# One batch's first keys and queries ahead of the last one's transposed maxima, three of four row copies on ScalarE, and layer 0's first loads on two queues

## The chip, the cores and the metric

The kernel runs on one core of one Trainium2 chip. The metric is the device time of one execution in microseconds (us), the median of several runs. Engines are named as in the profile: PE is TensorE's matmul queue, PEld its weight loads, DVE is VectorE, ACT is ScalarE, POOL is GpSimd, and SP is SyncE, which here only issues DMAs (SPq in rows).

## The reference, cut to what matters

```python
# layer 0: x (16, 256, 128), for each tile of 32 positions of every batch row
xn = layernorm(x)                       # the projections q, k, v, f, beta, gate from it
q, k, v = silu(x @ Wq), silu(x @ Wk), silu(x @ Wv)
f, gate = x @ Wf1 @ Wf2, x @ Wog1 @ Wog2
def step(S, inp):                       # 256 positions, one after the other
    bS = einsum('bhk,bhkv->bhv', b_t, S)
    S = exp(g)[..., None] * S + a_t[..., None] * bS[:, :, None, :] + k_t[..., None] * v_t[:, :, None, :]
    return S, einsum('bhk,bhkv->bhv', q_t, S)
# and 64 small experts with a group-limited router on the same normalised x
# layer 1: rotary queries and keys, 16 heads of 8, causal softmax attention per batch,
# and 16 experts with a top-3 router; out = x2 + silu(experts) * attention
```

## The kernel before

**Layer 0** works on eight tiles of 32 positions. For a tile, DVE makes a layer norm (`layer_norm`, stages 0 to 5), PE transposes it and `project` makes 648 columns of projections in 3-pass split matmuls (`split3`), units k = 0 to 5: unit 0 and 1 hold the narrow rest (136 columns) of four row blocks, unit 1 also the router's logits (12 matmuls of 64 columns), units 2 to 5 the 512 wide columns. ACT copies each unit into `zs`, SP stores it to HBM in 16 DMAs (`pass_z`) and loads it back in another layout (`zr`), ACT applies the nonlinearities (`recurrence_inputs`), DVE makes coefficients and then runs the 32 steps of the recurrence (`step`, nine DVE instructions each). Tile 0 has no earlier tile to hide its preparation behind. Ahead of it, PE transposes the factors `Wf1`, `Wog1` and multiplies them with `Wf2`, `Wog2` (semaphores `s_w1t_ps`, `s_w1t`, `s_w12_ps`), and DVE splits the projection weights `wp` and router weights `wr` in a high and a low part (`s_wp`). All loads stand on SP's queue, and PE, ACT and DVE wait for all 13 small ones (`s_small`) before anything else. DVE first widens the selectors `sel`, then splits the weights, then norms x. POOL splits the expert weights; from its fourth chunk on it waits for the prepared coefficients of tile 0 (`s_pq`), and SP's later chunk loads and the load of tile 1's x stand behind those splits in its order.

**Layer 1** first runs its experts in eight tiles. Then comes **attention**, one batch after the other, 16 in all, in a software pipeline written out by hand: the function `both(ba, bx, bo, ...)` stands on PE, ACT and DVE with the same places i = 0 to 17, and interleaves batch ba's keys, queries and row maxima (`a_unit`, the table `UNITS`), batch bx's transposed scores and exp (`scores_t`, `x_unit` at `X_AT`) and values (`values` at `V_AT`), and batch bo's output (`o_unit` at `O_TB` ... `O_END`). Each engine runs its list strictly in this order and waits on semaphores between.

- `k0`, `q0`, `k1`, `q1`: four matmuls each into banks 0 or 1; ACT copies the keys to `kr`, DVE the queries to `qr`; DVE masks keys (`masked_keys`), ACT masks queries (`masked_queries`, two ACTIVATEs at places 4, 7, 10, 13).
- `max` (12): scores in banks 2 and 3 for the row maxima, reduced by DVE.
- `v`: values' projection, from a copy of the latent (`ckv_b`) made by ACT at place 0.
- `m`: when the maxima are split (`mhl`), PE transposes them into banks 2 and 3, and four copies of 2 x 1024 elements (`max_rows`) put them into the queries' spare rows: two on ACT, then two on DVE (`s_mq`). The first `max` of the next batch and the first `scores_t` of this one wait for both.
- `scores_t` of one unit waits for the exp of the one before it (one bank pair); `values` 0 waits for the last output, `s_done`, which DVE signals at `O_END`.

Of the kernel before, what the change touches and what calls it, by code (L numbers as in the profile page):

```python
# [112 lines left out]
def layer0(nc, d, scratch, sem, area):  # L113

    z_dram, y_dram, g_dram = scratch
    with ExitStack() as ctx:
# [68 lines left out]
        s_small = sem("small_weights_loaded")  # L185
# [79 lines left out]
        SMALL = 13  # L265
# [9 lines left out]
        def _(sp):  # L275
# [37 lines left out]
            def pass_z(t, par, later):  # L313
# [21 lines left out]
            pass_z(0, 0, False)  # L335
# [178 lines left out]
        def _(act):  # L514
            act.wait_ge(s_eps, 2)

            act.wait_ge(s_small, SMALL * 16)
            act.activation(wp[:, :, ZB], wbeta[:, :], ACT.Copy).then_inc(s_w12, 1)
            act.wait_ge(s_w1t_ps, 1)
            act.activation(wf1T[:, :, :], pb[0:HD0, 0, 0:2 * P].rearrange("p (a b) -> p a b", a=2), ACT.Copy).then_inc(s_w1t, 1)  # L520
            act.wait_ge(s_w12_ps, 1)
            for a, at in ((0, ZF), (1, ZG)):
                act.activation(wp[:, :, at:at + HD0], pb[:, 2, D * a:D * (a + 1)].rearrange("p (h c) -> p h c", h=H0),
                               ACT.Copy).then_inc(s_w12, 1)

            def norm(t):

                act.wait_ge(s_xc, t + 1)
                act.activation(xn[:, :, :], xc[:, :, :], ACT.Square).then_inc(s_sq, 1)
                act.wait_ge(s_var, t + 1)  # L530
                act.activation(stat[:, 1, :], stat[:, 0, :], ACT.Sqrt, bias=eps[:, 0:1], scale=1.0 / D).then_inc(s_std, 1)

            def project(t, par, k, side):
# [10 lines left out]
                elif k == 1:  # L544
                    act.activation(zs[:, 3, WIDE:ZW], bank[:, 0:REST], ACT.Copy).then_inc(s_zc, 1)
                    act.activation(scores, bank[:, 256:512].rearrange("p (s e) -> p s e", s=NS), ACT.Sigmoid).then_inc(s_sc, 1)
# [35 lines left out]
            def tile(t, par, first, ahead):  # L582
# [3 lines left out]
                for r in range(SLOTS):  # L586
                    p, what = r // 3, r % 3
                    n = P if p < PAIRS else F0
                    if ahead and r == NORM_SLOT:
                        norm(t + 1)  # L590
# [25 lines left out]
            norm(0)  # L616
            for k in range(-1, UNITS):
                project(0, 0, k, k % 4)
# [15 lines left out]
        def _(pe):  # L634
# [15 lines left out]
            pe.wait_ge(s_wp, 4)  # L650

            def project(t, par, k, side):
# [15 lines left out]
                elif k == 1:  # L668
                    split3(bank[:, 0:REST], hi[:, sub[3]], lo[:, sub[3]], wp_hi[:, WIDE:ZW], wp_lo[:, WIDE:ZW])
                    for s in range(NS):  # L670
                        last = split3(bank[:, 256 + E0 * s:256 + E0 * (s + 1)], hi[:, sub[s]], lo[:, sub[s]], wr_hi[:, :], wr_lo[:, :], first=False)
# [1317 lines left out]
```

## Time and profile before

| | before |
|---|---|
| median of 3 runs | 2104.19 us (2104.09 to 2106.93) |
| the profiled execution: time, span | 2104.4 us, 2102.7 us |
| PE, DVE, ACT, POOL busy, share of the span | 78%, 76%, 54%, 48% |
| layer 0 up to the first recurrence step | 0 to 72.9 us |
| layer 0's tiles, layer 1's experts | to about 1178 us, to about 1721 us |
| attention, 16 batches | about 1722 us to the end |
| from one batch's transposed maxima on PE to the next one's | 22.07 us (1893.08 to 1915.15) |

A row of the timeline is: start us, duration us, engine, line, operation, out<-in, count of merged instructions, and in brackets how long the engine was idle before it and what released it. Where several instructions are merged, the duration runs to the end of the last one, so the distance to the next start is what one costs its engine. The 1.7 us between span and time lie outside of the profiled span.

### The profile page before, as it was taken

The numbers are of one execution on the slowest core, as the hardware profiler recorded it, in microseconds if no ns is written. First come the engines' busy times: TensorE is split into PE (matmuls) and PEld (weight loads), VectorE is DVE, ScalarE is ACT, GpSimd is POOL, SyncE is SP. The second block draws the span as 40 slices with busy tenths as digits, with TensorE's granted clock in tenths as the row PEclk, the third lists the DMA queues.
The fourth block names the chain that finished last, engine by engine and source line by source line (L and its number), as shares of the span: only waits on it lengthen the run. The fifth ranks groups of instructions, "written<-read, shape, count | busy, mean of one in ns | idle before, by whom it ended". The sixth has DMA issues, their size and how long they took to land. (4 is left out here: it accounts for less than half of the span.)

```text
span 2102.7 us, 32686 instructions
## 1 busy us (share of the span) xinstructions
PE 1635.4 (78%) x8418; PEld 1185.5 (56%) x8418; DVE 1603.5 (76%) x4329; ACT 1137.1 (54%) x1811; POOL 1018.5 (48%) x1108
## 2 busy tenths in 40 slices
PE   3286787886868768778787399898999997888886
PEld 2164454554545436445454298787988875555554
DVE  3499999999999999999999535444344457777774
ACT  1365464564645646546454154444555447777774
POOL 2577778686787877887887400000000002332332
PEclk9598898897978988989898599999999999999998
DMA  5420020110200202002001411001110010000000
GB/s 83 108 56 1 1 66 1 25 43 1 66 0 4 63 2 51 15 0 61 1 11 38 103 21 26 19 14 27 21 26 11 11 31 9 15 22 15 22 15 13
DMA packets 140707, 58.82 MB, mean 28 GB/s; under 512 B 94743, under 2 KB 135180, under 8 KB 140556
## 3 DMA queue, kind: packets, MB, share of 16 engines
q1 hardware_dynamic: 140556, 57.19, 12.1%
q8 instruction: 48, 0.79, 0.2%
q14 instruction: 103, 0.84, 0.1%
HBM read 36.05 MB, written 21.10 MB: 27 GB/s over the span
## 5 line engine op out<-in xcount | busy, mean ns | idle before, releaser
L612 ACT ACTIVATE shared_rings<-pb 128x512 f32<-128x512 f32 (+1 forms) x784 | 434.7, 598 | 360.6 <-PE pb L639 318.4
L688 PE MATMUL pb<-hid,shared_down 128*128 128x512 f32 x528 | 308.0, 669 | 159.7 <-POOL hid L490 157.1
L486 POOL TENSOR_TENSOR hid<-shared_rings 128x512 f32<-128x512 f32 x256 | 333.9, 1304 | 178.6 <-ACT shared_rings L612 164.2
L490 POOL TENSOR_TENSOR hid<-hid,shared_rings 128x512 f32<-128x512 f32 x256 | 329.6, 1288 | 20.6 <-POOL hid L486 1.0
L1818 DVE SCALAR_TENSOR_TENSOR l_acc<-l_pb,l_gtok,l_acc 128x128 f32<-128x128 f32 x512 | 144.3, 344 | 256.1 <-PE l_pb L1462 256.1
L637 PE MATMUL pb<-xt_hi,shared_hi 128*128 128x512 f32 (+1 forms) x264 | 192.3, 729 | 101.6 <-ACT shared_rings L612 101.6
L1373 ACT ACTIVATE l_hid<-l_pb,l_cols 128x512 f32<-128x512 f32 x256 | 169.3, 688 | 182.8 <-PE l_pb L1462 182.5
L1462 PEld LDWEIGHTS l_pb<-l_big,l_hid 128*128 128x128 f32 x2048 | 247.1, 192 | 10.6
L1462 PE MATMUL l_pb<-l_big,l_hid 128*128 128x128 f32 x2048 | 247.9, 275 | 0.0
L1287 POOL TENSOR_TENSOR l_ql<-l_rope,l_qh 128x512 f32 x8 | 10.3, 1286 | 459.4 <-ACT l_qh L1367 459.4
L688 PEld LDWEIGHTS pb<-hid,shared_down 128*128 128x128 f32 x528 | 101.1, 207 | 217.0 <-POOL hid L490 191.3
L1462 PE MATMUL l_pb<-l_xt,shared_hi 128*128 128x512 f32 x512 | 176.3, 426 | 19.7 <-DVE l_rope L1750 17.9
L950 DVE TENSOR_TENSOR products<-zr,rs 128x512 f32<-128x512 f32 x256 | 174.7, 682 | 10.2 <-issue 5.7
L953 DVE TENSOR_REDUCE rs<-products 128x32 f32<-128x512 f32 x256 | 176.0, 687 | 0.0
L951 DVE TENSOR_TENSOR products<-zr,rs 128x512 f32<-128x512 f32 x256 | 174.2, 681 | 0.0
L1861 DVE TENSOR_REDUCE l_mrow<-l_pb 128x2 f32<-128x512 f32 (+1 forms) x192 | 128.1, 687 | 58.8 <-PE l_pb L1462 58.4
L637 PEld LDWEIGHTS pb<-xt_hi,shared_hi 128*128 128x128 f32 (+1 forms) x264 | 54.4, 206 | 175.3 <-ACT shared_rings L612 88.1
L1299 POOL TENSOR_TENSOR l_turnstile<-l_turnstile 128x1 f32<-128x1 f32 x128 | 24.9, 195 | 254.3 <-ACT l_big L1421 189.6
L746 PE MATMUL pb<-cwt,sel 128*128 128x512 f32 x256 | 105.5, 412 | 19.2 <-ACT cwt L562 19.2
L638 PE MATMUL pb<-xt_lo,shared_hi 128*128 128x512 f32 (+1 forms) x264 | 112.4, 426 | 0.0
L639 PE MATMUL pb<-xt_hi,shared_lo 128*128 128x512 f32 (+1 forms) x264 | 111.8, 424 | 0.0
L637 PE MATMUL pb<-xt_hi,wu_hi 128*128 128x512 f32 (+1 forms) x264 | 111.2, 421 | 0.0
(319 smaller groups left out, 3803.7 us busy)
## 6 DMA issues: line engine op xcount, KB each, us to landing
z_scratch<-zs SPq DMA_DIRECT2D x128, 81.0 KB, 3.0
zr<-z_scratch SPq DMA_DIRECT2D x8, 1296.0 KB, 8.0
x_sb<-in_L_attn_x_dram SPq DMA_DIRECT2D x32, 64.0 KB, 2.0
shared_rings<-in_L_ffn_We_gate_dram SPq DMA_DIRECT2D x4, 512.0 KB, 5.8
shared_rings<-in_L_ffn_We_up_dram SPq DMA_DIRECT2D x4, 512.0 KB, 6.9
g_scratch<-zs SPq DMA_DIRECT2D x8, 256.0 KB, 2.8
y_scratch<-yo SPq DMA_DIRECT2D x8, 256.0 KB, 2.1
shared_down<-in_L_ffn_W_dram SPq DMA_DIRECT2D x4, 512.0 KB, 5.6
```

Source lines behind the costliest of these rows:

```text
L486: pool.tensor_tensor(hid1[:, :], g, u, ALU.mult).then_inc(s_h1, 1)
L490: pool.tensor_tensor(hid[:, (p + par) % 2, :], hid1[:, :], c, ALU.mult).then_inc(s_h, 1)
L612: act.activation(dst, pb[0:n, what, :], ACT.Silu if what == 0 else ACT.Copy).then_inc(s_ev, 1)
L637: pe.matmul(out, l_hi, r_hi, start=first, stop=False, skip_group_check=True)
L688: last = pe.matmul(pb[:, SUM, :], wd[0:n, p, :], hid[0:n, (p + par) % 2, :], start=(p == 0), stop=(p == PAIRS), skip_group_check=True)
L950: dve.tensor_tensor(products[:, 2:4], two(ZG), twice, ALU.mult).then_inc(s_st, 1)
L951: dve.tensor_tensor(products[:, 0:2], two(ZF), twice, ALU.mult).then_inc(s_st, 1)
L953: dve.tensor_reduce(rs[:, 3, 0:2], products[:, 2:4], AX.X, ALU.add).then_inc(s_st, 1)
L1373: act.activation(hid[:, r % HR, :], pb[:, 2 + r % 3, :], ACT.Relu, bias=cols[:, r:r + 1]).then_inc(s_hid, 1)
L1462: return pe.matmul(out, l, r, start=start, stop=stop, skip_group_check=True)
L1818: dve.scalar_tensor_tensor(out=acc[:, s, :], in0=pb[:, 5 + e % 2, sub], scalar=gtok[par][:, s, e:e + 1], in1=acc[:, s, :], op0=ALU.mult, o ...
L1861: dve.tensor_reduce(dst, pb[:, 2 + m % 2, :].rearrange("p (j n) -> p j n", j=heads), AX.X, ALU.max).then_inc(s_ua_dve, 1)
```

## The change

**Layer 0.** SP keeps x, the identity and the four factors (now `s_small`, five loads). ACT's queue issues the projection weights and beta (`s_heads`) and the router's constants (`s_late`), eight loads, as its first instructions. The layer norm of tile 0 goes first on DVE, then the weights' split, then `sel`. Tile 0's router matmuls come after all projections, into another bank, and ACT issues the last four of the 16 stores of `zs` itself, ahead of the router's sigmoid.

**Attention.** The unit `m` leaves the table: `max_transposed` (PE) and `max_in_queries` (ACT, DVE) now run at place 2 of the next call of `both`, behind `k0` and `q0` of the next batch. ACT copies three rows, DVE one. The latent's copy goes from place 0 to 14. The first `scores_t`/`x_unit` go from places 3 and 4 to 4 and 5 (`X_AT`), the first masked keys from 1 to 2, and the whole output unit one place on, `O_END` from 7 to 8.

```diff
-        SMALL = 13
+        SMALL, HEADS, LATE = 5, 4, 4
@@ sync: x, ident, wf1, wf2 stay; onehot, tri, bias64, gate_w, wp, wbeta go; pass_z(0, 0, False, True)
                     sp.wait_ge(s_zc, t * UNITS + (s + 3))
+                    if alone and s == NS - 1:
+                        continue
@@ scalar
+            for at, name in ((ZQ, "L0_attn_Wq"), (ZK, "L0_attn_Wk"), (ZV, "L0_attn_Wv")):
+                act.dma_start(wp[:, :, at:at + HD0], d[name].rearrange("i (h c) -> i h c", h=H0)).then_inc(s_heads, 16)
+            act.dma_start(wbeta[:, :], d["L0_attn_Wbeta"]).then_inc(s_heads, 16)
...
-            norm(0)
+            act.wait_ge(s_eps, 2)
+            norm(0, True)
+            head_weights()
             for k in range(-1, UNITS):
-                project(0, 0, k, k % 4)
+                project(0, 0, k, k % 4, True)
+            act.wait_ge(s_zc, UNITS)
+            for b in range(BS):
+                act.dma_start(z_dram[0, NS - 1, b].rearrange("h n c -> n h c"),
+                              zs[TP * b:TP * (b + 1), NS - 1, :].rearrange("p (h c) -> p h c", h=H0)).then_inc(s_zst, 16)
+            act.wait_ge(s_lg, 1)
+            router_scores(pb[:, SUM, :])
@@ vector
-            for stage in range(6):
+            for stage in range(5):
                 layer_norm(0, 0, stage)
+            head_weights()
+            layer_norm(0, 0, 5)
+            dve.wait_ge(s_late, LATE * 16)
+            dve.tensor_copy(sel[:, :, :], over(onehot[:, :], F0)).then_inc(s_sel, 1)
@@ layer 1, attention
-        UNITS = ["k0", "q0", "k1", "q1"] + ["max"] * 12 + ["v", "m"]
+        UNITS = ["k0", "q0", "k1", "q1"] + ["max"] * 12 + ["v"]
+        PLACES, MAX_AT, LATENT_AT, ROWS_BY_ACT = NU + 1, 2, 14, 3
-        QUERIES_AT, KEYS_AT = {4: (0, 0), 7: (0, 2), 10: (1, 0), 13: (1, 2)}, {1: (0, 0, 4), 5: (1, 0, 2), 7: (1, 2, 2)}
-        X_AT, V_AT = (3, 4, 6, 7, 9, 10, 12, 13), (9, 11, 14, 17)
-        RAW_AT, O_TB, O_NORM, O_OT, O_WO, O_END = 17, 1, 2, 4, 6, 7
+        QUERIES_AT, KEYS_AT = {4: (0, 0), 7: (0, 2), 10: (1, 0), 13: (1, 2)}, {2: (0, 0, 4), 5: (1, 0, 2), 7: (1, 2, 2)}
+        X_AT, V_AT = (4, 5, 6, 7, 9, 10, 12, 13), (9, 11, 14, 17)
+        RAW_AT, O_TB, O_NORM, O_OT, O_WO, O_END = 17, 2, 3, 5, 7, 8
@@ scalar
+            def max_in_queries(b, par):
+                act.wait_ge(s_mt, b + 1)
+                act.wait_ge(s_qb, (b + 1) * 4)
+                for j in range(ROWS_BY_ACT):
+                    last = act.activation(max_rows(par, j), pb[32 * j:32 * j + 2, 2:4, :].rearrange("p a (g n) -> p (a g) n", n=N), ACT.Copy)
+                last.then_inc(s_mq[0], 1)
...
-                for i in range(NU):
+                for i in range(PLACES):
                     if bo is not None:
                         o_unit(bo, i)
+                    if bx is not None and i == MAX_AT:
+                        max_in_queries(bx, px)
```

How the instructions stand shows on ACT at the turn from one batch to the next. Before, `l_pb` to `shared_hi` (line 1402) are the copies of the transposed maxima, `shared_down` to `l_big` is the latent, line 1393 copies keys 0 and keys 1, and line 1421 is the first exp:

```order
L1399 REGISTER_ALU
L1400 ISA [waits a_unit_in_psum]
L1402 ACTIVATE shared_hi<-l_pb 2x4x256 [waits a_queries_masked]
L1402 ACTIVATE shared_hi<-l_pb 2x4x256
L1389 ISA
L1389 ACTIVATE l_big<-shared_down 33x256
L1391 ISA
L1393 ACTIVATE l_wqk<-l_pb,shared_rings 128x512 [waits a_unit_in_psum]
L1391 REGISTER_ALU
L1393 ACTIVATE l_wqk<-l_pb,shared_rings 128x512 [waits a_unit_in_psum]
L1417 ISA
L1421 ACTIVATE l_big<-l_pb 128x768 [waits a_probs_used,a_scoresT_in_psum]
```

Now line 1429 is a copy of keys, line 1440 the three rows of maxima, line 1450 a masked query and line 1459 the first exp:

```order
L1427 ISA
L1429 ACTIVATE l_wqk<-l_pb,shared_rings 128x512 [waits a_unit_in_psum]
L1438 REGISTER_ALU [waits a_max_transposed]
L1440 ACTIVATE shared_hi<-l_pb 2x4x256 [waits a_queries_masked]
L1440 ACTIVATE shared_hi<-l_pb 2x4x256 x2
L1427 REGISTER_ALU
L1429 ACTIVATE l_wqk<-l_pb,shared_rings 128x512 [waits a_unit_in_psum]
L1446 ISA
L1450 ACTIVATE shared_lo<-l_xt,shared_rings 128x2x256 [waits a_unit_read_by_dve]
L1450 ACTIVATE shared_lo<-l_xt,shared_rings 128x2x256
L1455 ISA
L1459 ACTIVATE l_big<-l_pb 128x768 [waits a_probs_used,a_scoresT_in_psum]
```

Keys 0 stand ahead of the maxima and keys 1 behind them, the latent's copy is gone from here, and two masked queries now stand between keys 1 and the first exp.

On DVE the places 6 to 8 are these; lines 1861 and 1898 are the reductions of maxima, 1875 and 1920 masked keys, and the waits on `a_wo_in_psum` and after it are the output's last two operations. Before:

```order
L1848 REGISTER_ALU
L1861 TENSOR_REDUCE l_mrow<-l_pb 128x2 [waits a_unit_in_psum]
L1891 ISA [waits a_wo_in_psum]
L1892 TENSOR_TENSOR shared_rings<-l_pb,shared_rings 128x256 [waits a_gate1_loaded0]
L1895 REGISTER_ALU [waits a_x2_loaded0,a_final_chain]
L1896 TENSOR_TENSOR shared_rings<-shared_rings 128x256 [waits a_out_stored]
L1848 REGISTER_ALU
L1861 TENSOR_REDUCE l_mrow<-l_pb 128x4 [waits a_unit_in_psum]
L1875 TENSOR_SCALAR l_kb<-l_xt,shared_rings 128x2x256 [waits a_unit_read_by_act]
L1875 TENSOR_SCALAR l_kb<-l_xt,shared_rings 128x2x256
```

and now:

```order
L1885 REGISTER_ALU
L1898 TENSOR_REDUCE l_mrow<-l_pb 128x4 [waits a_unit_in_psum]
L1920 TENSOR_SCALAR l_kb<-l_xt,shared_rings 128x2x256 [waits a_unit_read_by_act]
L1920 TENSOR_SCALAR l_kb<-l_xt,shared_rings 128x2x256
L1936 ISA [waits a_wo_in_psum]
L1937 TENSOR_TENSOR shared_rings<-l_pb,shared_rings 128x256 [waits a_gate1_loaded0]
L1940 REGISTER_ALU [waits a_x2_loaded0,a_final_chain]
L1941 TENSOR_TENSOR shared_rings<-shared_rings 128x256 [waits a_out_stored]
L1885 REGISTER_ALU
L1898 TENSOR_REDUCE l_mrow<-l_pb 128x2 [waits a_unit_in_psum]
```

The output's last two operations have gone behind one more reduction and two masked keys.

On PE, behind the last values of a batch (line 1632 before, 1673 now), the transposes of the maxima are line 1588 before and 1650 now, `l_kh` to `l_ql` are keys 0 and queries 0 of the next batch. Before:

```order
L1588 MATMUL l_pb<-shared_rings,l_mhl 128x128 [waits a_max_split]
L1588 MATMUL l_pb<-shared_rings,l_mhl 128x128 x7
L1672 UNCONDITIONAL_BRANCH
L1672 ISA
L1462 ISA [waits a_unit_read_by_act]
L1462 MATMUL l_pb<-l_kh,l_rep 128x256
L1462 REGISTER_ALU
L1462 MATMUL l_pb<-l_kl,l_rep 128x256
L1462 MATMUL l_pb<-l_kh,l_rep 128x256
L1462 MATMUL l_pb<-l_kl,l_rep 128x256
L1639 REGISTER_ALU
L1643 MATMUL l_pb<-shared_rings,l_rope 128x128 [waits a_raw_out_copied]
```

and now:

```order
L1502 MATMUL l_pb<-l_kl,l_rep 128x256
L1502 MATMUL l_pb<-l_kh,l_rep 128x256
L1502 MATMUL l_pb<-l_kl,l_rep 128x256
L1625 REGISTER_ALU
L1502 REGISTER_ALU [waits a_unit_read_by_dve]
L1502 MATMUL l_pb<-l_qh,l_rep 128x256
L1502 REGISTER_ALU
L1502 MATMUL l_pb<-l_ql,l_rep 128x256
L1502 MATMUL l_pb<-l_qh,l_rep 128x256
L1502 MATMUL l_pb<-l_ql,l_rep 128x256
L1650 MATMUL l_pb<-shared_rings,l_mhl 128x128 [waits a_max_split]
L1650 MATMUL l_pb<-shared_rings,l_mhl 128x128 x7
```

Eight matmuls of the next batch now run ahead of the transposes, and keys 1 and the transposes of the raw output (`l_rope`) stand behind them.

## Rows read from the trace of the kernel before

**Rows 1.** Windows: busy time of each engine in one tile of layer 0.

```profile
211.00:349.00 138.00, 102.22 (x344) 66.15 (x344) 136.02 (x376) 76.90 (x129) 108.61 (x87) 0.87 0.11 26
```

**Rows 2.** Timeline of layer 0's start: loads, weights, layer norm, first projection.

```profile
9.15 0.66 SPq L295 DMA_DIRECT2D wbeta<-in_L_attn_Wbeta_dram  x1
...
11.44 2.29 DVE L780 CAST sel<-onehot 128x4096 fp32r<-128x4096 f32 x1 [10.21 <-DMA wbeta<-in_L_attn_Wbeta_dram]
...
15.05 0.85 DVE L783 CAST wp_hi<-products 128x648 fp32r<-128x648 f32 x1 [1.31 <-ACT products L523]
...
18.84 0.68 DVE L793 TENSOR_REDUCE rs<-x_sb 128x4 f32<-128x512 f32 x1
...
20.92 1.28 ACT L531 ACT_TABLE_LOAD   x1
...
26.20 0.45 PE L637 MATMUL pb<-wp_hi,xt_hi 128*128 128x136 f32 x1 [1.51 <-DVE xt_lo L810]
```

**Rows 3.** Timeline, the first wide projection, its stores and the load back.

```profile
31.31 0.77 PE L637 MATMUL pb<-wp_hi,xt_hi 128*128 128x512 f32 x1
...
34.03 8.36 SPq L322 DMA_DIRECT2D z_scratch<-zs  x16
...
47.95 0.56 SPq L325 DMA_DIRECT2D zr<-z_scratch  x1
...
56.12 0.65 ACT L567 ACTIVATE zr<-zr 128x512 f32<-128x512 f32 x1 [19.96 <-DMA zr<-z_scratch]
```

**Rows 4.** Timeline of DVE: the first recurrence step.

```profile
72.91 0.69 DVE L950 TENSOR_TENSOR products<-zr,rs 128x512 f32<-128x512 f32 x1
```

**Rows 5.** Timeline of ACT in one batch of attention, window from 1889 us.

```profile
1894.29 2.04 ACT L1402 ACTIVATE shared_lo<-l_pb 2x1024 fp32r<-2x1024 f32 x2 [0.39 <-PE l_pb L1588]
...
1898.32 0.69 ACT L1393 ACTIVATE l_xt<-l_pb,shared_rings 128x512 fp32r<-128x512 f32 x1 [0.83 <-PE l_pb L1462]
1898.91 0.80 ACT L1421 ACTIVATE l_big<-l_pb 128x768 f32<-128x768 f32 x1
1899.60 1.33 ACT L1412 ACTIVATE shared_hi<-l_xt,shared_rings 128x512 fp32r<-128x512 f32 x2
1900.82 0.81 ACT L1421 ACTIVATE l_big<-l_pb 128x768 f32<-128x768 f32 x1
1901.51 0.39 ACT L1432 ACTIVATE l_big<-l_pb 128x256 f32<-128x256 f32 x1
1902.33 0.81 ACT L1421 ACTIVATE l_big<-l_pb 128x768 f32<-128x768 f32 x1 [0.43 <-PE l_pb L1462]
```

**Rows 6.** Timeline of DVE in the same batch: output, reduction, masked keys.

```profile
1904.19 0.41 DVE L1892 TENSOR_TENSOR shared_rings<-l_pb,shared_rings 128x256 f32<-128x256 f32 x1
1904.74 0.42 DVE L1896 TENSOR_TENSOR shared_rings<-shared_rings 128x256 f32<-128x256 f32 x1
1905.08 0.68 DVE L1861 TENSOR_REDUCE l_mrow<-l_pb 128x4 f32<-128x512 f32 x1
1905.68 1.05 DVE L1875 TENSOR_SCALAR l_kb<-l_xt,shared_rings 128x512 fp32r<-128x512 f32 x2
```

**Rows 7.** Timeline of PE in the same batch.

```profile
1891.96 0.86 PE L1632 MATMUL l_pb<-l_front_rows,l_hid 128*32 128x256 f32 x16
1893.08 1.09 PE L1588 MATMUL l_pb<-shared_rings,l_mhl 128*128 128x128 f32 x8 [0.27 <-DVE l_mhl L1866]
...
1901.68 0.62 PE L1462 MATMUL l_pb<-shared_lo,l_wqk 128*128 128x512 f32 x2 [0.27 <-ACT l_big L1421]
1902.13 0.38 PE L1462 MATMUL l_pb<-shared_rings,l_big 128*128 128x128 f32 x2
...
1905.67 0.86 PE L1632 MATMUL l_pb<-l_big,l_hid 128*32 128x256 f32 x16
```

**Rows 8.** Attention's last stretch by windows, and PE's timeline in it.

```profile
2078.00:2084.00 6.00, 4.53 (x17) 3.53 (x18) 0.85 (x2) 2.71 (x4) 2.95 (x11) 0.54 0.00 0
...
2079.42 1.01 PE L1462 MATMUL l_pb<-shared_lo,l_wqk 128*128 128x512 f32 x2 [0.57 <-ACT l_big L1421]
```

The columns of a windows row are: the stretch, its length, then busy us and instructions of PE, PEld, DVE, ACT and POOL, the granted clock of PE, the busy share of the DMA engines and GB/s.

More of the change, by code:

```diff
@@ L514, in _ @@
         def _(act):
[L515 to L524, printed above, removed]
@@ L528, in norm, with router_scores @@
+            def norm(t, alone):
                 act.wait_ge(s_xc, t + 1)
                 act.activation(xn[:, :, :], xc[:, :, :], ACT.Square).then_inc(s_sq, 1)
+                if alone:
+                    factors()
                 act.wait_ge(s_var, t + 1)
                 act.activation(stat[:, 1, :], stat[:, 0, :], ACT.Sqrt, bias=eps[:, 0:1], scale=1.0 / D).then_inc(s_std, 1)
-            def project(t, par, k, side):
+            def router_scores(bank):
+                act.activation(scores, bank[:, 256:512].rearrange("p (s e) -> p s e", s=NS), ACT.Sigmoid).then_inc(s_sc, 1)
@@ L535, in project @@
+            def project(t, par, k, side, alone=False):
                 bank = pb[:, side, :]
@@ L545, in project @@
                     act.activation(zs[:, 3, WIDE:ZW], bank[:, 0:REST], ACT.Copy).then_inc(s_zc, 1)
-                    act.activation(scores, bank[:, 256:512].rearrange("p (s e) -> p s e", s=NS), ACT.Sigmoid).then_inc(s_sc, 1)
+                    if not alone:
+                        router_scores(bank)
                 else:
@@ L668, in project @@
                 elif k == 1:
-                    split3(bank[:, 0:REST], hi[:, sub[3]], lo[:, sub[3]], wp_hi[:, WIDE:ZW], wp_lo[:, WIDE:ZW])
-                    for s in range(NS):
-                        last = split3(bank[:, 256 + E0 * s:256 + E0 * (s + 1)], hi[:, sub[s]], lo[:, sub[s]], wr_hi[:, :], wr_lo[:, :], first=False)
+                    last = split3(bank[:, 0:REST], hi[:, sub[3]], lo[:, sub[3]], wp_hi[:, WIDE:ZW], wp_lo[:, WIDE:ZW])
+                    if not alone:
+                        last = router(par, bank, False)
                 else:
@@ L675, in project, with router @@
                 last.then_inc(s_zp, 1)
+            def router(par, bank, first):
+                for s in range(NS):
+                    sub = slice(P * s, P * (s + 1))
+                    last = split3(bank[:, 256 + E0 * s:256 + E0 * (s + 1)], xt_hi[par][:, sub], xt_lo[par][:, sub], wr_hi[:, :], wr_lo[:, :], first=first and s == 0)
+                return last
             def router_weights(t):
@@ L1658, in both @@
             def both(ba, bx, bo_, pa, px, po):
-                for i in range(NU):
+                for i in range(PLACES):
+                    if bx is not None and i == MAX_AT:
+                        max_transposed(bx)
                     if bx is not None and i in X_AT:
```

132 lines of the change are left out of this document (69 added, 63 removed).

## The prediction

> **What bounds the kernel now.** I read the stages first, by windows. In a tile of layer 0 DVE is busy 136.0 of 138 us [rows 1]: the recurrence sets that stage, so it ends as much sooner as its first step starts sooner, and nothing else there matters. Layer 1's experts are not touched. In attention no engine is full, so there the order of the instructions and their waits decide, and I followed one batch of the timeline on all three engines.
>
> The start is one serial chain. SP has issued its last small load at 9.15, and everybody waits for it: DVE's selectors start at 11.44 [rows 2]. DVE then splits the weights (15.05 to 18.8), only then norms x (from 18.84), and PE projects from 26.20 [rows 2]. The stores of the projections are issued from 34.03, the load back is issued at 47.95, when the last store has landed, and lands at 56.12, when ACT goes on after 20 us of idling [rows 3]. The first step stands at 72.91 [rows 4].
>
> A batch of attention has this chain. Values of the last batch on PE (1891.96), transposed maxima (1893.08) [rows 7], row copies on ACT (1894.29), two keys' copies, exp 0 at 1898.91, masked queries at 1899.60, exp 1 at 1900.82, the output's copy at 1901.51, exp 2 at 1902.33 [rows 5], the output's product on DVE at 1904.19 and its sum at 1904.74 [rows 6], and only after that sum the new values on PE at 1905.67 [rows 7]. Behind them in PE's order stand all remaining scores for maxima, which DVE needs to reach the next transposes. The same point comes again 22.07 us later (the table of times).
>
> **Layer 0's start.** x and the five factor loads stay ahead on SP. A small load is used 2.3 us after its issue begins (9.15 to 11.44) [rows 2]; x is issued first, before 2.7 us, so it is there at about 5.0. From 18.84 to 26.20 the norm, the transposes and their split take 7.4 [rows 2]. Put into that path are the split of the weights, 3.8 (15.05 to 18.84) less some 1.5 in which PE transposes x and ACT copies it anyway, so 2.3, and a table load of 1.3 ahead of ACT's first square (duration of the load at 20.92) [rows 2]; the selectors' 2.3 leave it. That gives 5.0 + 7.4 + 2.3 + 1.3 = 16.0 for the first projection, 10.2 sooner. ACT's queue was not used for loads before: if its eight issues cost what SP's cost, 0.7 each, they end at 6.4 and are early; if both queues shared one issuing unit, the factors would come as late as 11.4 as before, the first projection at about 19, 7.0 sooner. I take the first, since each engine's issues are instructions of its own.
>
> From 26.20 to 31.31 PE runs 24 narrow matmuls, 0.213 each [rows 2, 3]. Twelve of them, the router's, go behind the wide ones: 2.6 less before the first store, which is issued at 34.03 - 10.2 - 2.6 = 21.2. SP spends 8.36 on 16 issues, 0.52 each, and the last store lands 13.9 after the first issue [rows 3]. With four of them on ACT, SP's twelve end 2.1 sooner, so the load back is issued at 21.2 + 11.8 = 33.0. If the transfers and not the issues set the pace, this 2.1 is lost. The Trainium skill, DMA: Bandwidth & Descriptors (Issuing engines are not separate DMA queues), says just that: DMAs of all queues end on the same 16 engines and a second queue saves only the issuing time. By that rule alone the saving would be 12.8, by the row it is 14.9. I stay with 14.9. The load back takes 8.2 as before, so ACT goes on at 41.2 in place of 56.12: **14.9 us**. The router's sigmoid now comes behind ACT's four issues and the twelve matmuls, some 5 us of the 20 that ACT idled: hidden. Everything after (POOL's later splits, SP's chunk loads, tile 1's x) hangs on the coefficients of tile 0, so it moves along, and the first step is at 58.0. Bounds: 9.6 (shared issuing, 7.0 + 2.6, and nothing from the stores) and 17 (the last store lands 2 us sooner because fewer queue behind each other).
>
> **Attention.** I count from PE's values, 1891.96, as zero and move each step by pitches of the same rows. Before: transposes at 1.12, row copies 2.33, exp 0 6.95, exp 1 8.86, output copy 9.55, exp 2 10.37, product 12.23, new values 13.71.
>
> - Transposes: they waited for DVE's maxima until 1.12. Now the values (0.8 of PE) are followed by keys 0 and queries 0, eight matmuls. The nearest rows bound them by 0.4 (sixteen of the values' take 0.86) and 1.8 (two scores take 0.45, 1901.68 to 1902.13) [rows 7]; I take 1.1, between the two, as they have half the columns of a score: transposes at 1.9, so 0.8 later, row copies at 3.15.
> - Row copies on ACT: two took 2.04 [rows 5], three take 3.06 and end at 6.2. DVE's part shrinks by a row, but both counts are waited for, and ACT's is last. Before, ACT still had the latent's copy and keys 0 behind its rows, which are now elsewhere; keys 1 follow directly (pitch 0.6) and end at 6.8.
> - Exp 0 now has a masked pair of queries ahead of it, 1.22 (1899.60 to 1900.82) [rows 5]: 8.0 in place of 6.95, **1.05 later**. The three pieces nearly cancel up to there; what is left is the pair.
> - Exp 1: the next scores start 0.86 after an exp starts (1900.82 to 1901.68) and the exp 0.65 after that [rows 5, 7]. Before, this hid behind the masked pair; now it stands open: 8.0 + 1.5 = 9.5. Exp 2 the same, 11.0, 0.63 later than before.
> - The output's copy stood between exp 1 and exp 2, in ACT's idle time. At place 7 it comes behind exp 2: 11.0 + 0.69 = 11.7, **2.15 later**. Its matmuls on PE come 0.62 behind it (1901.51 to 1902.13) [rows 5, 7], at 12.3, and take 0.8.
> - DVE's product and sum, places 8 in place of 7, now wait for one more reduction and a masked pair of keys ahead of them: that reduction needs PE's matmul behind the output's, 13.1 + 0.75, then 0.6 and 1.0 [rows 6]: product at 15.45 (before 12.23), sum at 16.0, done at 16.45. The values, 13.71 before, start at 16.45, **2.75 later**. The fifth scores, just ahead of them on PE, come about 1 later, with exp 3, so they are not what is waited for.
> - Behind the values the order is as before. About 0.3 comes back, because DVE has already masked its keys when the next maxima are there. So the next batch's values come **2.45 us** later, 24.5 in place of 22.1.
>
> Fourteen calls of `both` carry all three batches: 14 x 2.45 = 34.3. In the first and the last ones the same places apply in part; I add 1.5. Attention: +36, bounds +28 and +42 by moving each of the pitches by a tenth.
>
> **Sum.** The profiled execution took 2104.4, as good as the median 2104.19. 2104.4 - 14.9 + 34.3 + 1.5 = **2125**. Its own range with the bounds above: 2104.4 - 17 + 28 to 2104.4 - 9.6 + 42, 2115 to 2137.
>
> **The rivals.**
> - *The output's delay is harmless* (other side). If the new values don't wait for the sum, because ACT or PE get there early by the moved latent copy and the earlier keys, only small changes are left in attention. For it: masked keys end about 1 us sooner, so the first maxima could start sooner. Against it: PE's list has the second scores ahead of the second maximum, and these wait for exp 0. Price: the head alone, 2089. It decides for faster as soon as a batch costs less than 1.05 more (14.9 / 14). Chance 0.17.
> - *Half of it*: a batch costs about 1.1 more, since only exp 0's delay remains: 2104.4 - 14.9 + 15.4 = 2105. Chance 0.07.
> - *PE's clock falls.* A batch would have three gaps of about 1.6 us (before the scores 0 and 1 and the values) where one was. In attention's last stretch, with such gaps, the granted clock is 0.54, mostly the lower level of 1.2 GHz, and a score pair takes 1.01 in place of 0.62 [rows 7, 8]. Each of some five rounds of scores and exp would cost 0.4 more, 2.0 a batch, 28 in all: 2153. The Trainium skill, TensorE: Matmul & The Clock Gate (Why this matters for your kernels), warns of idle gaps between bursts of matmuls, and the row agrees. Chance 0.14, and half-way cases are in the range.
> - *The start gives less*: one issuing unit for both queues, 9.6 us: 2131. Chance 0.1, inside of the main case's range.
> - The forecast, 2115 to 2137, has the remaining 0.52 and these 0.1.
>
> **How the numbers follow.** The likeliest is 2125. The range must leave out no more than 0.2: the first rival is left out, the half case and the fallen clock are taken in: 2100 to 2154. A measurement of this kernel tells about 0.2%, 4 us, from no change. Faster by more: 0.18; within: 0.05, from the half case; slower: 0.77.
>
> **What would show it.** Right: ACT's first nonlinearity on zr near 41 and the first step near 58; PE's transposed maxima 24 to 25 us apart from batch to batch; on PE the values of place 9 waiting for DVE's sum, with 1 to 2 us of idle time; ACT's output copy behind the third exp; an open gap of about 0.8 on ACT before exp 1 and exp 2. Wrong: a batch of 22 or less, values waiting for POOL or for nothing, or a load back that is issued later than 36.

## The result and the profile after

| | before | changed |
|---|---|---|
| median, 4 runs each on the same chip | 2105.56 us | 2144.03 us (2142.87 to 2147.72) |
| ratio | | 1.0186, 95% interval 1.0168 to 1.0203 |
| the profiled execution: time, span | 2104.4, 2102.7 us | 2143.75, 2141.7 us |
| first recurrence step of layer 0 | 72.91 | 61.17 |
| first transposed maxima of attention | 1736.34 | 1726.23 |
| mean distance of the 16 transposed maxima | 22.42 | 25.66 |

The kernel is 38.5 us slower; the forecast was 20.8 slower (2125 against 2104.2), with a range up to 2154. The page of the profile shows where to look. These are its busy time and its granted clock in 40 slices; the last eight slices are attention. The clock row of the kernel before stands below them.

```profile
span 2141.7 us, 32651 instructions
...
PE 1654.1 (77%) x8418; PEld 1203.1 (56%) x8418; DVE 1587.0 (74%) x4313; ACT 1152.2 (54%) x1827; POOL 1024.2 (48%) x1108
...
PEclk7697898988988889889896899999999988999997
```

```profile
PEclk9598898897978988989898599999999999999998
```

PE runs as many instructions as before (8418) and is busy longer with them (1654.1 against 1635.4 us), and the first two slices of attention have dropped to an eight. That is a hint, no more, as a nine covers everything from 0.90 up. The windows below show it plainly.

The timeline of the start, by the places of [rows 2 to 4]: layer norm on DVE, its table load on ACT, the first projection on PE, the first store on SP and the four on ACT's queue, the load back, ACT on zr, the first step.

```profile
6.11 0.69 DVE L822 TENSOR_REDUCE rs<-x_sb 128x4 f32<-128x512 f32 x1 [4.88 <-DMA x_sb<-in_L_attn_x_dram]
...
7.61 1.28 ACT L536 ACT_TABLE_LOAD   x1 [7.61 <-DVE xc L825]
...
16.67 0.45 PE L658 MATMUL pb<-wp_hi,xt_hi 128*128 128x136 f32 x1 [3.16 <-DVE xt_lo L839]
...
21.51 6.37 SPq L319 DMA_DIRECT2D z_scratch<-zs  x12
...
24.75 2.02 ACTq L636 DMA_DIRECT2D z_scratch<-zs  x4
...
36.13 0.67 SPq L322 DMA_DIRECT2D zr<-z_scratch  x1
...
44.37 0.65 ACT L580 ACTIVATE zr<-zr 128x512 f32<-128x512 f32 x1 [15.91 <-DMA zr<-z_scratch]
...
61.17 0.69 DVE L979 TENSOR_TENSOR products<-zr,rs 128x512 f32<-128x512 f32 x1
```

Up to the first store the sum is nearly as forecast (21.51 against 21.2). From there to the load back it takes 14.6 us, not the 11.8 of the forecast and not less than the 13.9 of before [rows 3]. The load back is issued at 36.13, just past the 36 that the forecast had named as a sign of being wrong. The first step is 11.7 sooner, not 14.9.

One batch of attention, by the places of [rows 5 to 7]. First ACT's timeline: row copies, keys 1, masked pair, exp 0, 1 and 2, the output's copy.

```profile
1908.15 3.07 ACT L1440 ACTIVATE shared_lo<-l_pb 2x1024 fp32r<-2x1024 f32 x3 [0.47 <-PE l_pb L1650]
1911.25 0.69 ACT L1429 ACTIVATE l_xt<-l_pb,shared_rings 128x512 fp32r<-128x512 f32 x1
1911.84 1.32 ACT L1450 ACTIVATE shared_hi<-l_xt,shared_rings 128x512 fp32r<-128x512 f32 x2
1913.06 0.80 ACT L1459 ACTIVATE l_big<-l_pb 128x768 f32<-128x768 f32 x1
1914.72 0.81 ACT L1459 ACTIVATE l_big<-l_pb 128x768 f32<-128x768 f32 x1 [0.86 <-PE l_pb L1502]
1916.63 0.81 ACT L1459 ACTIVATE l_big<-l_pb 128x768 f32<-128x768 f32 x1 [1.10 <-PE l_pb L1502]
1917.33 0.38 ACT L1470 ACTIVATE l_big<-l_pb 128x256 f32<-128x256 f32 x1
```

Then DVE's: masked keys, the output's product and its sum.

```profile
1920.16 1.13 DVE L1920 TENSOR_SCALAR l_kb<-l_xt,shared_rings 128x512 fp32r<-128x512 f32 x2
1921.21 0.41 DVE L1937 TENSOR_TENSOR shared_rings<-l_pb,shared_rings 128x256 f32<-128x256 f32 x1
1921.75 0.65 DVE L1941 TENSOR_TENSOR shared_rings<-shared_rings 128x256 f32<-128x256 f32 x1
```

And PE's: the last values of the batch before (the zero of the count), the transposed maxima, scores 0, 1, 2 and 3, the new values, and the next transposed maxima.

```profile
1905.16 0.86 PE L1673 MATMUL l_pb<-l_front_rows,l_hid 128*32 128x256 f32 x16
...
1907.00 1.03 PE L1650 MATMUL l_pb<-shared_rings,l_mhl 128*128 128x128 f32 x8
...
1911.36 0.61 PE L1502 MATMUL l_pb<-shared_lo,l_wqk 128*128 128x512 f32 x2 [1.50 <-ACT shared_lo L1440]
...
1913.91 0.77 PE L1502 MATMUL l_pb<-shared_lo,l_wqk 128*128 128x512 f32 x2 [1.48 <-ACT l_big L1459]
...
1915.58 1.01 PE L1502 MATMUL l_pb<-shared_lo,l_wqk 128*128 128x512 f32 x2
...
1917.49 0.67 PE L1502 MATMUL l_pb<-shared_lo,l_wqk 128*128 128x512 f32 x2 [0.23 <-ACT l_big L1459]
...
1922.55 0.86 PE L1673 MATMUL l_pb<-l_big,l_hid 128*32 128x256 f32 x16 [2.25 <-DVE shared_rings L1941]
...
1932.36 1.03 PE L1650 MATMUL l_pb<-shared_rings,l_mhl 128*128 128x128 f32 x8
```

The three gaps on PE are there: 1.50 and 1.48 ahead of scores 0 and 1, and one ahead of the values, which DVE's sum ends, as forecast. That third gap is 2.25 in this batch and 1.90 in the 13 other batches from the second on. The kernel before has 1.54 and 0.66 and none ahead of the values. Scores 2 take 1.01 where a pair at full clock takes 0.61. The windows of the same stretch (the last but two number is the granted clock) say why:

```profile
1911.00:1913.00 2.00, 1.07 (x4) 0.58 (x4) 1.93 (x6) 1.98 (x4) 0.00 (x0) 1.00 0.00 0
1913.00:1915.00 2.00, 1.09 (x5) 1.03 (x5) 0.16 (x1) 1.14 (x3) 0.90 (x3) 0.80 0.00 0
1915.00:1917.00 2.00, 2.00 (x7) 1.15 (x6) 1.19 (x3) 0.90 (x2) 0.90 (x3) 0.50 0.00 0
1917.00:1919.00 2.00, 1.77 (x13) 1.44 (x11) 0.99 (x2) 2.00 (x5) 0.90 (x3) 0.84 0.00 0
...
1939.00:1941.00 2.00, 1.74 (x6) 1.34 (x6) 0.00 (x0) 0.91 (x2) 0.90 (x3) 0.50 0.00 0
1941.00:1943.00 2.00, 1.84 (x6) 1.04 (x5) 1.60 (x4) 0.90 (x3) 0.90 (x3) 0.50 0.00 0
1943.00:1945.00 2.00, 1.92 (x8) 1.83 (x9) 0.57 (x1) 2.00 (x5) 0.91 (x3) 0.52 0.00 0
```

Around the second gap the granted clock falls to 0.50, the 1.2 GHz level, and then returns to 2.4 GHz. In this batch that is so in one whole window and parts of two, in the next batch in nearly all of three windows. The distance to the next transposed maxima is 25.4 in the first case and 26.0 in the second (1932.36 to 1958.33); all but two of the 15 distances lie between 25.0 and 26.1, one at 27.9 and the first at 24.6. The clock falls in all 15.

The trace of before had a case of this that the forecast did not use. In 3 of its 15 batches the clock falls as well: the first takes 24.39, the ninth 22.98 and the last 24.15, where the usual one takes 22.07. The ninth, from 1915.15 on, shows it:

```profile
1919.00:1921.00 2.00, 1.40 (x10) 1.31 (x10) 1.97 (x5) 1.17 (x3) 0.00 (x0) 1.00 0.00 0
1921.00:1923.00 2.00, 1.34 (x7) 1.08 (x5) 1.61 (x5) 2.00 (x5) 0.91 (x3) 0.62 0.00 0
1923.00:1925.00 2.00, 2.00 (x8) 1.14 (x7) 0.82 (x2) 0.97 (x2) 0.91 (x3) 0.53 0.00 0
```

### The profile page after: what moved, and what is told of

Its sections match the earlier page's. It is cut to its first block and busy times, and to the rows that moved or that the text cites. A ratio compares the mean times of both kernels' runs of the same rounds, so it can differ in the third digit from the quotient of the medians.

```text
span 2141.7 us, 32651 instructions
## 1 busy us (share of the span) xinstructions
PE 1654.1 (77%) x8418; PEld 1203.1 (56%) x8418; DVE 1587.0 (74%) x4313; ACT 1152.2 (54%) x1827; POOL 1024.2 (48%) x1108
## 3 DMA queue, kind: packets, MB, share of 16 engines
q1 hardware_dynamic: 135692, 56.53, 11.7%
## 5 line engine op out<-in xcount | busy, mean ns | idle before, releaser
L994 DVE TENSOR_TENSOR rs<-part,rs 128x256 f32<-128x256 f32 x256 | 108.5, 424 | 3.7
```

## The experiments

Each kernel was measured together with the kernel before on the same chip. That one's median was 2098.4 beside the first four (head_alone to out_early), 2098.6 beside the next four and 2105.1 beside the last four, so compare ratios. "Batch" is the mean distance of the 16 transposed maxima on PE (before: 1736.34 to 2072.62, changed: 1726.23 to 2111.06, 15 distances each), "clock" the granted clock in the window from 1750 to 2040 us. Both come from one profiled execution each, which was not always a typical one: rows22's took 2121.0 (median 2126.9), out_mid's 2123.2 (median 2117.9).

| kernel | median | ratio (95%) | batch | clock |
|---|---|---|---|---|
| before | | 1 | 22.42 | 0.99 |
| changed | 2144.03 | 1.0186 (1.0168 to 1.0203) | 25.66 | 0.89 |
| head_alone | 2088.93 | 0.9957 (0.9945 to 0.9969) | 22.32 | 0.99 |
| attn_alone | 2150.27 | 1.0244 (1.0227 to 1.0261) | 25.76 | 0.88 |
| stores_sp | 2089.84 | 0.9953 (0.9937 to 0.9970) | 22.40 | 0.98 |
| out_early | 2139.53 | 1.0189 (1.0172 to 1.0206) | 25.68 | 0.88 |
| rows22 | 2126.85 | 1.0140 (1.0107 to 1.0172) | 24.82 | 0.91 |
| exp_early | 2120.04 | 1.0108 (1.0074 to 1.0142) | 24.39 | 0.98 |
| filled | 2122.08 | 1.0102 (1.0074 to 1.0131) | 24.54 | 1.00 |
| both_early | 2093.00 | 0.9972 (0.9958 to 0.9986) | 22.55 | 0.95 |
| out_mid | 2117.86 | 1.0060 (1.0039 to 1.0081) | 23.95 | 0.91 |
| filled_mid | 2096.90 | 0.9970 (0.9955 to 0.9985) | 22.67 | 1.00 |
| both_rows22 | 2089.78 | 0.9927 (0.9906 to 0.9947) | 22.06 | 0.96 |
| best2_filled | 2077.01 | 0.9867 (0.9840 to 0.9895) | 21.38 | 1.00 |

**The two halves apart: head_alone and attn_alone.** The first is the changed layer 0 with the attention of before, the second the other way round; no line is new.

> Layer 0 of the changed kernel with the attention of the kernel before. In the changed kernel's trace the first step stands at 61.17 where it was 72.91. Theory: that distance of 11.7 is carried through all of layer 0 and layer 1 unchanged, 2105.6 - 11.7 = 2094. Rival A: part of it is lost at the passage to layer 1 or in front of attention, 2098 to 2105. Rival B: the forecast's 14.9 is reached when attention is as before, 2091.

> Layer 0 of the kernel before with the attention of the changed kernel. Theory: the two parts add up, so attention alone costs 38.5 + 11.7 = 50.2: 2156, transposed maxima 25.7 apart in the mean. Rival: the parts share something (POOL's or SP's queues at the end of layer 1), and attention alone costs the forecast's 36: 2141.

Attention alone costs 51.9 us (2150.3 - 2098.4), the head alone saves 9.5 (interval 6.5 to 11.5). Their sum is 42.4 and the product of their ratios 1.0200, inside the interval of the change (1.0168 to 1.0203), so within some 4 us the parts add up; the rival of 36 for attention fell. The head's 9.5 is short of the 11.7 of its theory, which lies just outside of the interval, and the forecast's 14.9 (rival B) fell. In the traces of this pair the first step is at 60.30 in place of 72.25, and the first transposed maxima at 1723.07 in place of 1733.53: 12.0 sooner at the start, 10.5 at attention. The 1.5 between the two can't be told from scatter: over the 14 traces the stretch from the first step to the first transposed maxima takes between 1657.5 and 1668.0 us.

**The stores: stores_sp.** Against head_alone:

```diff
-            pass_z(0, 0, False, True)
+            pass_z(0, 0, False)
...
-            act.wait_ge(s_zc, UNITS)
-            for b in range(BS):
-                act.dma_start(z_dram[0, NS - 1, b].rearrange("h n c -> n h c"),
-                              zs[TP * b:TP * (b + 1), NS - 1, :].rearrange("p (h c) -> p h c", h=H0)).then_inc(s_zst, 16)
```

> As head_alone, but the four stores of the last piece of the projections go back from ACT's queue to SP's, so that SP issues all 16. Theory: the transfers and not the issues set when the last store has landed, so the load back is issued at 36.1, within 0.7, as with four of them on ACT, and the time is that of head_alone within 1 us. Rival, the forecast's: the issues set the pace, the load back is issued 2.1 later than in head_alone, at 38.2, and the first step comes 2.1 later.

The issues in its trace, all on SP's queue, and the load back:

```profile
21.66 8.01 SPq L319 DMA_DIRECT2D z_scratch<-zs  x16
...
34.45 0.68 SPq L322 DMA_DIRECT2D zr<-z_scratch  x1
```

The time is that of head_alone, as expected. SP issues for 8.0 us and yet the load back comes 12.8 behind the first store; with four stores on ACT it was 13.6 in head_alone and 12.5 to 14.7 in all eleven traces that have them. The load back at 34.45 is earlier than the 36.1 within 0.7 that I had expected, and 0.8 sooner than in head_alone (35.27), but that is inside the scatter just given. The second queue buys nothing that shows: the issuing ends 4.8 us before the load back, which waits for the last store (21.66 + 8.01 against 34.45). The Trainium skill, DMA: Bandwidth & Descriptors (Issuing engines are not separate DMA queues), states that starting DMAs on several engines saves only the time it takes to start them, and the trace agrees. The 2.1 us of the forecast are not there.

**The output's places: out_early.** Against the changed kernel:

```diff
-        RAW_AT, O_TB, O_NORM, O_OT, O_WO, O_END = 17, 2, 3, 5, 7, 8
+        RAW_AT, O_TB, O_NORM, O_OT, O_WO, O_END = 17, 1, 2, 4, 6, 7
```

> The changed kernel with the output's five places put back to 1, 2, 4, 6 and 7; the transposed maxima, the three rows on ACT and the places of the exponentials stay changed. Theory: the values wait for the output's sum, so most of the batch's loss is this term; the output's copy comes back behind exp 1 and the values some 2 sooner, what is left is exp 0's delay of 1.05: 2144 - 15 x 2.2 = 2111. Rival: the late exponentials and PE's clock set the batch by themselves, the wait for the sum only fills their idle time: 2138 to 2144.

It gains nothing: 1.0189, as the rival had it. Taken alone this would have refuted the forecast's main term. The timeline of PE, with the last values, the transposes of the raw output (L1684) and the transposed maxima (L1650), shows what took its place:

```profile
1925.59 0.86 PE L1673 MATMUL l_pb<-l_front_rows,l_hid 128*32 128x256 f32 x16
...
1927.59 1.09 PE L1684 MATMUL l_pb<-shared_rings,l_rope 128*128 128x128 f32 x8 [0.48 <-ACT l_rope L1464]
...
1929.00 1.03 PE L1650 MATMUL l_pb<-shared_rings,l_mhl 128*128 128x128 f32 x8
```

With O_TB at 1 the raw output's transposes stand ahead of the maxima in PE's order and wait for ACT's copy. The maxima are transposed 3.41 behind the values, in the changed kernel 1.84. The edit gave back one delay and put in another; out_mid below takes the second one out again.

**The clock: filled.** Matmuls whose result nobody reads are added in PE's idle time. PE also waits, ahead of the values' group, until DVE has read the bank that the last eight of them write (the last two lines).

```diff
+            def idle(n, bank):
+                for _ in range(n):
+                    mm(pb[:, bank, :].rearrange("p (j n) -> p j n", j=4), ident_b[:, :], mask_b[:, :].unsqueeze(1).to_broadcast([P, 4, P]))
...
                 if u == 0:
+                    pe.wait_ge(s_pt, b * XU)
+                    idle(5, 4)
                     for n in range(2):
                         pe.wait_ge(s_mq[n], b + 1)
+                if u == 1:
+                    idle(6, 3)
...
                 if g == 0:
+                    idle(8, 3)
                     pe.wait_ge(s_done, b)
...
+                    if bx is not None and i == V_AT[0] and ba is not None:
+                        pe.wait_ge(*read(ba, 7))
```

> The changed kernel with matmuls added in PE's idle time of each batch whose result nobody reads: 5 ahead of the first scores, 6 ahead of the second, 8 ahead of the values of place 9 (each 512 columns, some 0.22 at full clock, 4.2 in all, in gaps of 1.50, 1.48 and 2.25). Theory that the clock takes part: the granted clock in attention rises from 0.89 to 0.95 or more, scores and maxima of the stretch after the gaps take 0.61 and not 0.77 to 1.01, and the batch gets 0.4 to 0.8 shorter: 2132 to 2138. Rival: the clock doesn't matter as PE waits anyway, or the added matmuls delay the scores as much: 2144 or more; what it says of the clock is then read from the windows.

The changed kernel gets 0.8% faster by more work (ratio 1.0186 to 1.0102), more than I had expected: 1.0102 of 2105.6 is 2127, 5 to 11 below the 2132 to 2138 expected. One batch by its window, and from PE's timeline its last values of the batch before, scores 1, the added matmuls ahead of the values, the values and the next zero:

```profile
1896.00:1921.00 25.00, 23.01 (x177) 14.67 (x175) 16.09 (x30) 17.93 (x26) 7.87 (x24) 1.00 0.05 16
```

```profile
1894.87 0.86 PE L1682 MATMUL l_pb<-l_front_rows,l_hid 128*32 128x256 f32 x16
...
1903.62 0.62 PE L1502 MATMUL l_pb<-shared_lo,l_wqk 128*128 128x512 f32 x2 [0.25 <-ACT l_big L1459]
...
1909.44 1.90 PE L1502 MATMUL l_pb<-l_mask_b,l_ident_b 128*128 128x512 bf16 x8
...
1911.30 0.86 PE L1682 MATMUL l_pb<-l_big,l_hid 128*32 128x256 f32 x16
...
1919.26 0.86 PE L1682 MATMUL l_pb<-l_front_rows,l_hid 128*32 128x256 f32 x16
```

The clock stays at 1.00 and, but for the first and the last distance (27.5 and 23.7), every batch is 24.4 long. So the order alone costs 24.4 - 22.1 = 2.3, and the clock the other 1.1 (means: 25.66 - 24.54). The added matmuls end just when the values may start, so they don't hold them up by more than 0.1: the values stand at 16.43 behind the zero where the forecast, which had none, put 16.45.

**Rows and exponentials: rows22, exp_early, both_early.** Against the changed kernel, one edit each, both_early with the last two:

```diff
-        PLACES, MAX_AT, LATENT_AT, ROWS_BY_ACT = NU + 1, 2, 14, 3
+        PLACES, MAX_AT, LATENT_AT, ROWS_BY_ACT = NU + 1, 2, 14, 2
```

```diff
-        X_AT, V_AT = (4, 5, 6, 7, 9, 10, 12, 13), (9, 11, 14, 17)
+        X_AT, V_AT = (3, 4, 6, 7, 9, 10, 12, 13), (9, 11, 14, 17)
```

```diff
-        RAW_AT, O_TB, O_NORM, O_OT, O_WO, O_END = 17, 2, 3, 5, 7, 8
+        RAW_AT, O_TB, O_NORM, O_OT, O_WO, O_END = 17, 2, 3, 4, 6, 7
```

> The changed kernel with two of the four row copies on ACT and two on DVE, as before. ACT's three took 2.99 in the trace (1908.15 to 1911.14) and keys 1, the masked queries and exp 0 follow on ACT without a gap. Theory: the third row's 1.0 lies on the chain to exp 0 and from there to the output's sum, so a batch gets 0.8 to 1.0 shorter: 2144 - 15 x 0.9 = 2130. Rival: DVE, which has the second keys' masks to do, gets late with two rows (2 x 1.0 there), and nothing is gained: 2142 to 2146.

> The changed kernel with the first two scores and exponentials back at places 3 and 4, in front of the first pair of masked queries on ACT. Theory: exp 0 comes 1.2 sooner and hides the pair, the output's copy behind exp 2 comes about 0.7 sooner: 2144 - 15 x 0.7 = 2133. Rival: the masked queries are now later for the maxima, and DVE's maxima set the batch: no gain, 2142 to 2148.

> The changed kernel with exponentials 0 and 1 back at places 3 and 4 and the output's places at 2, 3, 4, 6 and 7 (its copy and its sum one place sooner than in the change, the transposes of the raw output one later than before). Theory: both delays named in the forecast are gone, the batch costs no more than before (22.1 to 22.5), so what is left is the saving of layer 0: 2094, bounds 2090 to 2100. Rival: three rows on ACT and the earlier projections still cost 1 us a batch: 2109.

rows22 is as the theory had it: 0.84 off a batch, and its ratio interval holds the expected 2130 (1.0116). exp_early gives more than expected, 1.27. Only part of that is the order: a batch of it at full clock is 23.9 (1938.67 to 1962.57 in PE's timeline), 0.5 under filled's 24.4. The rest goes with the clock, 0.98 in place of 0.89. PE's timeline there, scores 0 and 1:

```profile
1943.02 0.61 PE L1502 MATMUL l_pb<-shared_lo,l_wqk 128*128 128x512 f32 x2 [1.97 <-ACT shared_lo L1440]
...
1944.61 0.62 PE L1502 MATMUL l_pb<-shared_lo,l_wqk 128*128 128x512 f32 x2 [0.52 <-ACT l_big L1459]
```

The second gap has shrunk from 1.48 to 0.52, and the clock falls in 6 of the 15 batches in place of all 15. But the sizes of the gaps alone don't say when it falls: both_early has the same 1.97 and 0.52, and without exp_early's third gap of 1.90, and it falls in 9 of 15; rows22 has 0.92, 1.00 and 1.90, and it falls in all. Why exp_early was spared nine times in a row no run here shows. both_early is faster than before by 0.3%, as far as the intervals tell the same as head_alone (0.9958 to 0.9986 against 0.9945 to 0.9969); the rival of 2109 fell.

**The output's term, clean: out_mid and filled_mid.** out_mid is the changed kernel with the last diff above alone; filled_mid has the added matmuls ahead of scores 0 and 1 too.

> The changed kernel with the output's places at 2, 3, 4, 6 and 7: the transposes of the raw output stay behind the transposed maxima, but the output's copy is at place 6 again, ahead of exp 2, and its product and sum at place 7. In out_early the first place had gone back too, and there PE put the raw output's transposes ahead of the transposed maxima, which came 3.4 behind the values in place of 1.8. Theory: that 1.6 had eaten the gain of out_early, and the output's delay does cost: a batch 1.5 to 2 shorter than 25.7, 2144 - 15 x 1.7 = 2118. Rival: the sum is not what the batch waits for, and out_mid stays within 3 us of the change, 2141 to 2147.

> As out_mid, with 5 and 6 matmuls added ahead of the first and the second scores (none ahead of the values), so that the clock does not fall. With the filled gaps the change had a batch of 24.4 at granted clock 1.00, as the forecast had it for full clock (24.5). Theory: at full clock the output's delay by one place is 1.5 of these, so a batch is 22.9 to 23.2 here, the rest being exp 0's delay of 1.05: 2122 - 15 x 1.3 = 2102. Rival: 24.4 as in filled, exp 0 and the third row set it: 2122.

out_mid takes 1.7 off a batch, as expected, and its transposed maxima come 1.84 behind the values, as in the changed kernel. At full clock the pair is filled and filled_mid, 24.4 and 22.64 (1906.41 to 1929.05). In filled_mid's timeline DVE's sum and PE's values follow each other as before:

```profile
1940.53 0.42 DVE L1949 TENSOR_TENSOR shared_rings<-shared_rings 128x256 f32<-128x256 f32 x1
...
1941.46 0.86 PE L1681 MATMUL l_pb<-l_big,l_hid 128*32 128x256 f32 x16
```

PE now goes on to the values without idle time, where the changed kernel waits 1.9 us for the sum. So the output one place later costs 1.75 us a batch, and out_early had hidden it. The same order without and with added matmuls (2117.9 and 2096.9, measured together) gives the clock's price a second time: 21 us, 1.28 a batch. filled_mid's theory held (2102, a ratio of 0.998 against 0.9970), and its rival of 2122 fell.

**A faster kernel: both_rows22 and best2_filled.** both_early with ROWS_BY_ACT at 2, and the same with idle(4, 4) ahead of the first scores.

> As both_early (exponentials 0 and 1 at places 3 and 4, output at 2, 3, 4, 6, 7) with two row copies on ACT and two on DVE. rows22 took 0.8 off a batch of the change. Theory: with two rows the first gap of PE (1.97 in both_early) shrinks by 1.0 and the batch by 0.4 to 0.8, also since the clock falls less often: 2093 - 15 x 0.5 = 2085. Rival: with exp 0 early the rows are no longer what is waited for, DVE's two rows delay the masked keys: 2092 to 2100.

> As both_rows22 with 4 matmuls of 512 columns added ahead of the first scores, in PE's idle time. Theory: granted clock 0.99 to 1.00 in attention, and where both_rows22 has batches of the longer kind (with the half clock, 0.9 longer in both_early) they are as short as the others: 3 to 7 us faster than both_rows22, about 2080. Rival: the gap is already short enough for the clock, and the matmuls add nothing or up to 0.3 a batch: 2085 to 2090.

both_rows22 takes 0.5 off a batch, as expected; its 2089.8 is above the 2085 named, but the kernel before was slower beside it too (2105.1), and its ratio of 0.9927 is near what the same theory makes of both_early's (0.9972 less 7.5 us, 0.9936). best2_filled is 12.8 us faster than both_rows22 where 3 to 7 were expected, 1.3% faster than before (interval 1.05 to 1.6%) and 3.1% faster than the changed kernel (0.9867 / 1.0186 = 0.969). both_rows22 has batches of 21.4 and of 22.5 to 22.9 in turn, and the long ones are those in which the clock falls. The filled one has only 21.4, but for the first two and the last:

```profile
1898.79 1.03 PE L1654 MATMUL l_pb<-shared_rings,l_mhl 128*128 128x128 f32 x8
...
1920.21 1.04 PE L1654 MATMUL l_pb<-shared_rings,l_mhl 128*128 128x128 f32 x8
```

## Why the prediction was right in kind and too small

The step that failed is the sum of attention: it was added up at full clock, and the fall of PE's clock stood at nothing in it. The runs show 1.1 to 1.3 us a batch for it, about 17 us in all; the forecast was 18 short. A second term, the stores of layer 0, was mis-sized by 2.1. Right were the direction, the place of the loss and the order of events. Counted from the last values, the steps of the forecast, of the changed kernel, and of filled, where the clock stays up:

| step | before | forecast | changed | filled |
|---|---|---|---|---|
| exp 0 | 6.95 | 8.0 | 7.90 | 7.90 |
| exp 1 | 8.86 | 9.5 | 9.56 | 9.40 |
| exp 2 | 10.37 | 11.0 | 11.47 | 10.95 |
| output's copy | 9.55 | 11.7 | 12.17 | 11.65 |
| output's product | 12.23 | 15.45 | 16.05 | 15.38 |
| values | 13.71 | 16.45 | 17.39 | 16.43 |
| whole batch | 22.07 | 24.5 | 25.0 to 26.1 | 24.4 |

- **Attention at full clock**, +2.45 a batch: filled has +2.3, and no step of the walk is off by more than 0.1. Its parts were also weighed apart: output one place later 1.75 (filled to filled_mid), exponentials 0 and 1 behind the masked pair 0.5 to 0.65 (filled's 24.4 to the 23.9 of exp_early's full-clock batches, filled_mid's 22.64 to the 22.0 of both_early's), the third row on ACT 0.6 (22.0 to 21.4, both_early to both_rows22, full-clock batches). Together 3.0 at most, of which the rest of the edit gives 0.65 back (21.4 against 22.07). That last figure is a difference and was not tried by itself. The forecast had said that the third row, the moved latent copy and the earlier keys nearly cancel; in sum they did, though the row alone costs 0.6. One reading of its walk was off without harm: before the change the values did not wait for DVE's sum, which was done at 1905.16 [rows 6], 0.5 ahead of them, and PE had no idle time there.
- **The failed step: "PE's clock falls" stood among the rivals at 0.14, as a case for itself.** The gaps of about 1.6 were in the forecast's own walk, and with them the clock fell in every batch; with the gaps filled it did not (filled). The two cases were one: forecast order and lower clock. Its price was given as 2.0 a batch, 28 in all; measured are 1.1 to 1.3 a batch, 17 (15 x 1.12) in the changed kernel and 21 in the order of out_mid. Only some of the scores, and the maxima between them, run slow in a batch, not five rounds. The 22.98 of the kernel before, 0.9 above its neighbours, was the nearer row for the price. The Trainium skill, TensorE: Matmul & The Clock Gate (Why this matters for your kernels), warns of idle gaps between bursts; those that this section names are longer than PE's here (2.25 at most from the second batch on, 2.97 in the first), so here the measurement decides: shorter gaps close together were enough.
- **Layer 0's start**, -14.9: measured -11.7 at the first step and 9.5 in time (6.5 to 11.5). x landed at 6.1 and not 5.0, so the first projection came 9.5 sooner and not 10.2; the first store was nearly on time; the 2.1 for four stores on ACT were wrong (stores_sp), and the other 0.7 between 14.6 and 13.9 is inside the scatter of that stretch (12.5 to 14.7). The sentence beside the term, that by the page's rule alone the saving would be 12.8, was nearer.
- **The ends**: +1.5; the first transposed maxima are 10.1 sooner where the first step was 11.7 sooner, and behind the last ones it takes 30.6 in place of 30.1. So 2.2, which happens to be near: the larger part, 1.6, lies in a stretch that scatters by 10 us from trace to trace.

The sum in the two traces: -10.1 until the first transposed maxima, +48.5 over 15 distances, +0.6 behind, which is the 39.0 between the two spans. Of the 48.5, 17 is the clock (15 x 1.12) and 32 the order. The forecast's sum had 20.8; it lacked 17 for the clock and 3 at the start, and 2 were too much elsewhere. That the time still fell inside the range of 2100 to 2154 is due to the range having taken in the clock's case at its too high price of 2153.

## What to carry to other kernels

When a forecast opens idle gaps on PE, the price of the clock belongs into the same sum, not beside it as a rival: look for the batches of the old trace in which the clock already fell, and take the price from them. An undone edit that changes nothing is no proof that the edit was free; read what waits now, since a place in a fixed order moves past several queues at once. And where the last store lands long after the last issue, as here, a second issuing queue saves nothing; the row of the load that waits for the stores tells at once.

## What the runs showed of the hardware

- PE's granted clock fell to its 1.2 GHz level in batches with idle times of 0.9 to 2.4 us, though not in all of them, and cost 1.1 to 1.3 us a batch where it fell in all or nearly all. The counts, each from one trace:

| kernel | usual idle times of PE over 0.6 us in a batch, from the second on | batches of 15 in which the clock fell |
|---|---|---|
| changed | 1.50, 1.48, 1.90 | 15 |
| rows22 | 0.92, 1.00, 1.90 | 15 |
| out_early | 2.37, 1.26 | 15 |
| out_mid | 1.50, 1.02 | 14 |
| both_early | 1.97 (and one of 0.4 to 0.5) | 9 |
| both_rows22 | 1.40 (and one of 0.4 to 0.5) | 8 |
| exp_early | 1.97, 1.90 (and one of 0.4 to 0.5) | 6 |
| before | 1.54, 0.66 | 3 |
| filled, filled_mid | none | 1, the first |
| best2_filled | none | 0 |

- Matmuls nobody reads, put into those gaps (4 to 19 a batch of 512 columns, 0.22 us each), held it at 1.00 from 1750 to 2040 us. The kernel with 4 a batch measured 2077.0 beside 2089.8 without them, measured together.
- The time from the first of 16 stores to the landing of the last was 12.5 to 14.7 us with two issuing queues, and with one 12.8 in stores_sp and 13.6 and 13.9 in the two traces with layer 0 as before. It is read from the first issue to the issue of the load back, which waits for the last landing.
